# A two-layer decoder on one core: item 0 of the mixture stage routed inside cross attention, and ScalarE's copies in that stage reordered

## The reference

```python
x = _layernorm(x + _L1_xattn_ref(x, ctx_2048, ctx_2048), axis=-1)      # cross attention, 8 heads
x = _layernorm(x + _L1_ffn_ref(x, router_w, shared_gate, ...), axis=-1)  # mixture of 8 experts, top 2

def _L1_ffn_ref(x, ...):                  # I = 176 columns an expert
    g, u = flat @ shared_gate.T, flat @ shared_up.T
    shared_out = jax.nn.sigmoid(g) * u @ shared_down.T
    weights = jax.nn.softmax(flat @ router_w.T, axis=-1)
    top_w, top_idx = jax.lax.top_k(weights, 2)
    comb = jnp.zeros_like(weights).at[jnp.arange(N)[:, None], top_idx].add(top_w)
    ge = jnp.einsum('nh,eih->nei', xb, wg)   # bfloat16
    ue = jnp.einsum('nh,eih->nei', xb, wu)
    he = jax.nn.sigmoid(ge) * ue
    de = jnp.einsum('nei,ehi->neh', he, wd)
    routed = (comb[:, :, None] * de).sum(axis=1)
    return x + shared_out + routed
```

## Time and profile before

| | |
|---|---|
| median of 3 runs | 1069.96 us (1065.61 to 1076.04) |
| the profiled execution | 1073.17 us, span 1071.4 us |
| mean granted clock of TensorE | 0.969 |
| busy: PE, DVE, ACT, POOL | 976.2, 881.8, 639.2, 527.8 us |
| last stage, shared columns of item 2 to those of item 15 | 950.84 to 1049.49 us |

### The profile page before, as it was taken

One profiled execution on the slowest core, in us unless ns is written; L12 is line 12 of the kernel. 1 busy time (PEld: TensorE's weight loads), 2 busy tenths in 40 slices (PEclk: granted clock), 3 DMA queues, 4 the chain that ended last, 5 costly groups with the idle time before them and its releaser, 6 DMA issues. The chain is left out here.

```text
span 1071.4 us, 25367 instructions
## 1 busy us (share of the span) xinstructions
PE 976.2 (91%) x8561; PEld 731.2 (68%) x8610; DVE 881.8 (82%) x2034; ACT 639.2 (60%) x1627; POOL 527.8 (49%) x983
## 2 busy tenths in 40 slices
PE   5789899878999769999999999999988999879996
PEld 4557676655666358888888888888865666456664
DVE  3479899777999787999999999998664999668885
ACT  3345555538999535555555555555534999835553
POOL 4277778865555532444444444444332556432332
PEclk8799999999999999999999999999997999989999
DMA  9999978964764300140000000004003566212121
GB/s 180 198 185 202 197 125 137 153 152 108 175 167 131 98 25 11 26 101 23 24 23 24 24 24 28 18 19 117 21 13 86 153 165 168 80 31 60 46 60 35
DMA packets 95584, 96.84 MB, mean 90 GB/s; under 512 B 11825, under 2 KB 86241, under 8 KB 95201
## 3 DMA queue, kind: packets, MB, share of 16 engines
q1 hardware_dynamic: 91680, 83.69, 35.5%
q10 hardware_dynamic: 3344, 9.38, 2.9%
q0 software_dynamic: 432, 2.16, 1.1%
HBM read 64.78 MB, written 19.99 MB: 79 GB/s over the span
## 5 line engine op out<-in xcount | busy, mean ns | idle before, releaser
L431 DVE TENSOR_REDUCE ca_nm<-p_p 128x2 f32<-128x512 f32 x256 | 163.3, 677 | 13.9 <-PE p_p L321 12.6
L576 ACT ACTIVATE ca_pt<-p_p 128x512 f32<-128x512 f32 x256 | 142.6, 598 | 11.2 <-PE p_p L340 5.8
L2031 ACT ACTIVATE la_pq<-p_p,la_nm 128x128 f32<-128x128 f32 x256 | 90.3, 366 | 37.6 <-DVE la_nm L2153 37.6
L340 PE MATMUL p_p<-ca_qs,ca_ks 128*128 128x256 bf16 x512 | 100.5, 279 | 6.0 <-ACT ca_qs L568 2.4
L321 PE MATMUL p_p<-ca_ks,ca_qs 96*128 96x256 bf16 x512 | 99.4, 278 | 2.1 <-DVE ca_nm L431 2.1
L72 POOL TENSOR_TENSOR ca_pt<-la_lt,one 64x1024 f32<-64x1024 f32 x32 | 60.4, 1889 | 58.9 <-ACT la_lt L2010 57.7
L568 ACT ACTIVATE ca_qs<-p_p 32x1024 bf16<-32x1024 bf16 x64 | 65.1, 1017 | 22.4 <-PE p_p L330 20.9
L2015 ACT ACTIVATE la_qq<-p_p 128x512 f32<-128x512 f32 x32 | 19.1, 597 | 99.0 <-PE p_p L1825 99.0
L1856 PE MATMUL p_p<-ca_pt,la_qq 128*128 128x128 f32 x512 | 70.9, 282 | 0.5 <-POOL ca_pt L72 0.3
L356 PE MATMUL p_p<-ca_pt,ca_va 128*32 128x256 f32 x1024 | 68.9, 386 | 0.0
L1111 DVE TENSOR_REDUCE sa_nm<-p_p 128x4 f32<-128x512 f32 x64 | 43.7, 685 | 30.4 <-PE p_p L969 30.3
(11 more groups left out here) (269 smaller groups left out, 2725.4 us busy)
## 6 DMA issues: line engine op xcount, KB each, us to landing
sa_qks<-sa_qkp SPq DMA_DIRECT2D x96, 128.0 KB, 5.8
ca_qs<-q_parts SPq DMA_DIRECT2D x32, 192.0 KB, 3.2
ca_ks<-k_parts SPq DMA_DIRECT2D x32, 192.0 KB, 3.6
ca_qs<-q_parts SPq DMA_DIRECT2D x32, 128.0 KB, 3.2
ca_ks<-k_parts SPq DMA_DIRECT2D x32, 128.0 KB, 3.6
ca_ct<-in_ctx_t SPq DMA_DIRECT2D x32, 128.0 KB, 3.5
ca_xr<-x_state SPq DMA_DIRECT2D x32, 128.0 KB, 2.1
x_state<-ca_xn SPq DMA_DIRECT2D x32, 128.0 KB, 2.0
```

Source lines behind the costliest of these rows:

```text
L340: last = pe.matmul(p_e[n % 2][:, kc, :], KS[b % 4][:, h, 128 * kc:128 * kc + 128], QS[b % 4][:, h, :], start=True, stop=True)
L431: dve.tensor_reduce(NM[b % 2][:, h, :], p_s[n % 3][:, :, :], AX.X, ALU.max, negate=True).then_inc(max_done, 1)
L576: act.activation(PT[g][:, j, :, :], p_e[n % 2][:, :, :], ACT.Exp, scale=SCALE).then_inc(exp_done, 1)
L2031: last = act.activation(PQ[g % 2][:, j, :], p_s[g % 2][:, j, :], ACT.Exp, bias=NM[b % 2][:, 4 * g + j:4 * g + j + 1], accum_out=SM[g % 2][ ...
```

## The change

It does five things.

- **ScalarE, steady state.** `copy_x` of the next item comes ahead of sigmoid 0. The copy of the shared columns leaves `copy_inner`, becomes `copy_shared(b)`, and is issued one item later, between sigmoid 0 and sigmoid 1; for item 15 it is issued at the very end. The count of its semaphore stays two an item.
- **VectorE.** `route` of item 0 comes ahead of its `inner_shared`; `shift_logits` of item 0 waits for the matmul only, not for the sigmoid.
- **TensorE at the seam.** `turn_x` of item 0 is issued behind slot 118, where it was behind slot 122; `shared` of item 0 behind slot 119, where it was behind slot 122.
- **VectorE at the seam.** `copy_xb` of item 0 is issued behind slot 120 (it was behind 121), `shift_logits` of item 0 behind slot 122 and `route` of item 0 behind slot 124 (both were behind the whole of cross attention).
- **GpSimd and ScalarE at the seam.** `power` of item 0 is issued behind slot 123 (it was behind all of cross attention), `copy_x` of item 0 behind slot 118 (it was behind 122).

```diff
@@ tensor(pe) of the mixture stage
         pe.wait_ge(older["max_done"], 8 * 2 * B)
         turn_x(0, 0)
+        yield "turned"
         shared(0, 0)
@@ scalar(act)
-        def copy_inner(b, part):
-            wait(act, inner_turned, 2 * b + part + 1)
+        def copy_inner(b):
+            wait(act, inner_turned, 2 * b + 1)
             wait(act, ret_ready, b)
-            if part == 0:
-                act.activation(HET[:, 0:8, :], p_h[:, :, :], ACT.Copy).then_inc(inner_copied, 1)
-            else:
-                act.activation(HET[:, 8:CHUNKS, :].rearrange("p k s -> p (k s)"),
-                               p_k[:, 256:448].bitcast(BF16), ACT.Copy)
-                act.activation(HST[:, :, :], p_k[:, 0:256].rearrange("p (c s) -> p c s", c=2),
-                               ACT.Copy).then_inc(inner_copied, 1)
+            act.activation(HET[:, 0:8, :], p_h[:, :, :], ACT.Copy).then_inc(inner_copied, 1)
+            wait(act, inner_turned, 2 * b + 2)
+            act.activation(HET[:, 8:CHUNKS, :].rearrange("p k s -> p (k s)"),
+                           p_k[:, 256:448].bitcast(BF16), ACT.Copy)
+
+        def copy_shared(b):
+            act.activation(HST[:, :, :], p_k[:, 0:256].rearrange("p (c s) -> p c s", c=2),
+                           ACT.Copy).then_inc(inner_copied, 1)
@@ scalar(act), pair
-                sigmoid(b, 0)
                 if later:
                     copy_x(b + 1)
+                sigmoid(b, 0)
+                if not is_first(b):
+                    copy_shared(b - 1)
                 sigmoid(b, 1)
                 if later:
                     sigmoid_shared(b + 1)
                 sigmoid(b, 2)
                 sigmoid(b, 3)
-                copy_inner(b, 0)
-                copy_inner(b, 1)
+                copy_inner(b)
 
         for i in range(PAIRS):
             yield from pair(i)
+        copy_shared(B - 1)
@@ vector(dve)
         def shift_logits(b):
-            wait(dve, shared_sig, b + 1)
+            if is_first(b):
+                wait(dve, shared_ready, b + 1)
+            else:
+                wait(dve, shared_sig, b + 1)
...
         shift_logits(0)
+        yield "shifted"
+        route(0, 0)
+        yield "routed"
         inner_shared(0)
-        route(0, 0)
@@ gpsimd(pool)
         power(0)
+        yield "powered"
@@ two_layers, tensor
-            until(three, 122)
+            until(three, 118)
+            until(four, "turned")
+            until(three, 119)
             until(four, 0)
             until(three, "weighed")
@@ two_layers, vector
-            until(three, 121)
+            until(three, 120)
             until(four, "copied")
+            until(three, 122)
+            until(four, "shifted")
+            until(three, 124)
+            until(four, "routed")
             until(three)
@@ two_layers, gpsimd
             until(four, "started")
+            until(three, 123)
+            until(four, "powered")
             until(three)
```

## The result

The changed kernel takes 1061.32 us (median of 20 runs, 1058.07 to 1067.16), the kernel before in the same sessions 1070.22 us (20 runs, 1065.61 to 1076.04). The ratio is 0.9925, with a 95% interval of 0.9908 to 0.9941: 8.0 us faster by the ratio (the medians lie 8.9 apart), inside the forecast range, under 1%, and less than the 10.8 us forecast.

What follows compares the result with a forecast made beforehand. TensorE's 7.59 us beat, with a 0.68 us wait for copy_x, and a 4.17 us entry gap were taken as the bound. Gains of 6.5 (head), 4.0 (13 periods) and 0.3 (tail) made 10.8: 1069.96 to 1059.2 us, range 1054.5 to 1065.5.

Steps and rivals of the forecast that it cites:

- The steady period: Mixture stage, S to S of successive items: 7.28 us against 7.59, a gain of 0.31 an item.
- The feared 0.04: Steady state: spare time in us between the transposes' end and copy_x's new start, counting 13 times if lost.
- both loops: Steady state: one loop over copy_x, one over sigmoid 0 and product 1 to unit 3, the latter forecast at 7.28 us.
- The case in which the steady gain is lost: Steady state: copy_x waits, delaying sigmoid 0 and unit 3; 0.3 us per item lost, 1063.2 us; chance 0.19.
- the one with TensorE alone: Steady state: TensorE alone binds, unit 3 does not wait; 8.1 us gained instead of 4.0, 1055.1 us; chance 0.10.
- the term of 0.3: Tail, item 15: sigmoid of unit 0 takes the moved shared copy's place, gaining 0.3 us.
- The third loop: Steady state: S through shared gate, shift, power, routing, residual and shared product to next S; about 7.2 us, under 7.28.
- The head: Mixture stage entry, items 0 and 1: early routing removes TensorE's gap, bringing S of item 2 6.5 us sooner.
- case 4 of the rivals: Items 0 and 1: the clock falls all the same; 1.6 us lost, 1060.8 us; chance 0.12.

Runs made afterwards that it cites:

- The two experiments on ScalarE's order: Changed kernel with the shared-column copy back in its old place: 1066.92 us; changed kernel with sigmoid 0 ahead of copy_x, shared-column copy behind both: 1064.38 us.
- filling the waits: Changed kernel plus 30 transposes nobody reads, in TensorE's two waits at the seam: 1062.25 us, ratio 0.9893; once more: 1060.87 us, ratio 0.9906.
- two reorderings on VectorE: Changed kernel with product 1 ahead of normalisation and cast: 1060.29 us; the same with the logits' shift also ahead of the cast: 1056.91 us.

## Why the prediction was right, and where it was off

**The steady period was right.** 7.28 was worked out and 7.30 measured (unit 3 is at 994.55, and in the chain of the next item at 1001.85). Each step shows: `copy_x` takes the slot of the shared copy (1.29 behind the first copy), sigmoid 0 does not move, the wait at S falls and one of 0.33 at unit 3 comes up. The feared 0.04 between the transposes and `copy_x` held: the transposes end at 991.74, the copy starts at 991.86. The two experiments on ScalarE's order show that both loops exist with the lengths given. The case in which the steady gain is lost is out, and so is the one with TensorE alone.

**The sum of periods and tail was a little high.** I had 4.0 for the 13 periods and 0.3 for the last item. From S of item 2 to the end the gain is 120.56 - 116.57 = 3.99. The table of stages splits it as 4.08 and -0.08, for two reasons that nearly cancel: the first period gains 0.61, as unit 3 of item 1 does not wait yet, and behind S of item 15 stands the new wait at unit 3 of item 14. Counted from that unit 3 to the end, 20.00 us before and 19.75 after, the tail gains 0.25, so the term of 0.3 was nearly right. Most of the missing 0.3 is 0.02 in each of 13 periods.

**The third loop was named, and its second exit missed.** I had it from the shared product to the next S, at about 7.2. It bound at 7.20 once unit 3's wait was taken away, but by way of the residual and the transposes, which share a bank. The exit that I named, from the shared product to S, is there as well and holds S back by 0.10, yet it does not close: the shift has 0.22 to spare behind it.

**The head: the price was right, and its condition held in some executions.** S of item 1 was put at 938.3, 16.5 behind the last maxima; it is at 16.67 (16.48 to 16.77 over three profiles). The 0.2 are in ScalarE's stand: 2.27 us, not 2.0, as the last weight load landed 4.1 us after issue and not 3.9, and S of item 0 ran into it. From S of item 1 to S of item 2 I had 6.0 with a full clock: two profiles show 5.90, the third 7.54. That third is case 4 of the rivals, put at a price of 1.6 and a chance of 0.12; the price is right (1.6), the chance too low: it came in five of nine profiles, namely in each of the nine whose clock was at 1.00 from 119 to 112 us ahead of the last maxima. The step that failed is the sentence that with the gap gone the longest stand of about 1.3 us is short enough. By the Trainium skill (TensorE: Matmul & The Clock Gate, Part 1) the gate goes by how busy TensorE has been lately. The table of stretches of the changed kernel fits that, with a fall after 1.00 and 1.02 us of waiting near each other.

**The sum.** Worked out: 10.8. In profiles with a full clock 149.60 - 139.20 = 10.4 and 10.7; with the fall 8.8. The one profile of the kernel before is of the sort of the first two, so 10.4 and 10.7 compare like with like. In medians, where executions of both sorts are probably mixed, 8.9 and 9.6 us in the two sessions that had both kernels (1070.22 to 1061.32, 1071.49 to 1061.93); the interval of the first ratio, 0.9908 to 0.9941, means 6.3 to 9.8.

What stays open: whether filling the waits always prevents the fall, and what, in two executions of one program, decides both it and the clock 119 us ahead of the maxima.

## What to carry to other kernels

Before moving an instruction up, write down every loop that closes through the same engine, with its length: moving one ahead in a queue moves another back, and the gain ends where the next loop binds (0.62 us to be had, 0.29 got, and 0.28 more by two reorderings on VectorE). Two engines' work that shares a bank makes a loop of its own, and a wait put down to "issue" can be it. When executions differ upstream of a change, measure it in profiles from a fixed point ahead of it: the last maxima came between 912.08 and 922.81 us in the same code, and behind them the profiles of one kernel with one clock agreed within 0.4 us (139.20 and 138.93, 138.71 and 139.11).

## What the runs showed of the hardware

TensorE's clock may fall to 1.2 GHz without any wait longer than 1.02 us, when two such waits stand close together, and in the next execution of the same kernel it may not. One fall was worth 1.6 us here, and behind the 4.17 us gap of the kernel before the clock fell as well. In eleven profiles with unfilled waits the fall at S of item 1 came just in the six whose clock stood at 1.00, and not at 0.50, from 119 to 112 us ahead of the last maxima.
